# One level of Strassen's algorithm in both feed-forward stages of a chain of transformer layers

## The chip, the cores and the metric

The kernel is one program on 1 core of one Trainium2 chip. The metric is the device time of one execution in microseconds, the median of several runs. TensorE (PE) multiplies, VectorE (DVE), ScalarE (ACT) and GpSimd (POOL) compute elementwise, SyncE (SP) issues most transfers. Everything is fp32.

## The reference

Batch B = 16, T = 128 rows, width D = 512. Seven blocks follow one another: self attention, cross attention, a feed-forward stage, a grouped attention, a recurrence, an attention over latents, a second feed-forward stage. The change touches the two feed-forward stages alone, each of which is, with a hidden width of 2048:

```
x = rows of the block before                   # (16, 128, 512)
h = gelu(norm(x) @ w1 + b1)                    # (16, 128, 2048)
out = residual + h @ w2 + b2                   # (16, 128, 512)
```

The first one (`mlp`) has a layer norm and its own rows as the residual, the second (`pmlp`) an RMS norm and another tensor as the residual.

## The kernel before

Both stages are built by `mlp_phase` (L1908), called at L3282 as `mlp` and at L3298 as `pmlp`. A stage takes the 16 sequences two at a time, so it has NIT = 8 iterations; `run_iterations` writes out the first and the last and puts the six between into a loop. Each engine has its own program, with the order written out by hand; semaphores tie them together. `W1` and `W2` lie in SBUF (`region_a`) for the whole stage.

An iteration on PE (`body`, L2073): first the hidden products (L2083). For each of 16 tiles of 128 hidden features, four matmuls add up over the 512 inputs. Weights of 128x128 are the stationary operand, the 256 rows of both sequences the moving one. Two tiles share a bank, four banks go round (`Ring` `ph`). ScalarE takes each bank through gelu into `h_t` (L2013). Then PE transposes the normed rows of the next iteration (L2069), which ScalarE writes as `src_t` (L2004, `rows_features`). Then the output products (L2095): for each of the two sequences 16 matmuls with a 128x128 tile of `h_t` stationary and 512 columns of `W2` moving. VectorE adds bank and residual into `y` (L2050), SyncE stores it (`store`).

VectorE also norms the rows of the next iteration (`normalise`, L2024: statistics at L227 to L241, then L2034 or L2037), with the reciprocal root on GpSimd (L247, `rstd_on_pool`). GpSimd adds `b2` to the residual (L1986). `first.x` holds the rows of a stage's first iteration, prepared by the stage before. ScalarE starts the loads of the next stage's weights at the very beginning of a stage (L1996); those of the stage behind `mlp` go to `region_b` (`D_w`). `own_weights.wait` waits for the stage's own. Elsewhere the rows speak of the recurrence (L2915: products of 128x128 weights with 128 columns; L2404, L2700, L2714: elementwise work of GpSimd and VectorE) and of the group stage (L1764, L1801).

## Time and profile before

| | |
|---|---|
| median of 3 runs | 3412.55 us (3410.26 to 3412.62) |
| profiled execution | 3415.04 us, span 3413.3 us, mean granted TensorE clock 0.974 |
| PE busy | 3159.8 us, 93% of the span |
| VectorE, ScalarE, GpSimd busy | 1738.8, 1165.0, 865.6 us |
| `mlp` stage | about 717 to 1172 us of the span |
| `pmlp` stage | about 2957 us to the end |

In the rows, L12 is line 12 of the kernel. A group gives its engine, operation, output and inputs, shapes, count, the busy time in us, the mean duration of one in ns, and the time in which its engine stood idle ahead of it, with what ended that. Each fp32 matmul shows as two records of PE and two of PEld (the weight load). Neighbours in a pipeline overlap, so a mean duration is longer than the distance from one start to the next. PEclk is the granted TensorE clock as a share of 2.4 GHz.

### The profile page before, as it was taken

To read this page: it belongs to the slowest core of one execution; us is meant where nothing else is said; L and a number is where in the kernel's file an instruction comes from. 1 tells how busy PE (TensorE), PEld (TensorE's weight loads), DVE (VectorE), ACT (ScalarE), POOL (GpSimd) and SP (SyncE) were. 2 spreads that over 40 slices of the span, in tenths; PEclk is the share of its full clock that TensorE was granted. 3 is DMA by queue.
4 is the path that set the end of the run, shared out by engine and by line. 5 is a ranking of instruction groups with operands and counts; after the bars stand their busy time and mean duration, and the time that the engine had idled before them with its cause. 6 is when DMAs were issued, how large, how long until landed. Compare 5 with 4: busy or idle time off the path is not lost. (4 is left out here: it accounts for less than half of the span.)

```text
span 3413.3 us, 52562 instructions
## 1 busy us (share of the span) xinstructions
PE 3159.8 (93%) x19136; PEld 2073.7 (61%) x19136; DVE 1738.8 (51%) x2498; ACT 1165.0 (34%) x4115; POOL 865.6 (25%) x629
## 2 busy tenths in 40 slices
PE   8999899989999989886899999997899999899999
PEld 5665566656666655554676667664455555567675
DVE  5555455520000078884899999997344644400000
ACT  3444233431111176662343444342233433311110
POOL 3333233310000012222655555555000000100000
PEclk9999999989999999997999999998899999999999
DMA  4110231110000131111111111110231110101010
GB/s 170 43 43 27 83 130 52 40 62 25 15 22 15 42 147 53 52 33 66 45 39 41 47 50 38 44 42 29 74 125 34 38 32 24 47 22 34 22 34 12
DMA packets 104306, 170.16 MB, mean 50 GB/s; under 512 B 16512, under 2 KB 54016, under 8 KB 100736
## 3 DMA queue, kind: packets, MB, share of 16 engines
q1 hardware_dynamic: 99296, 124.58, 11.5%
q10 hardware_dynamic: 4896, 44.04, 3.2%
q8 instruction: 74, 1.21, 0.1%
q14 instruction: 40, 0.33, 0.0%
HBM read 135.03 MB, written 33.55 MB: 49 GB/s over the span
## 5 line engine op out<-in xcount | busy, mean ns | idle before, releaser
L2404 POOL TENSOR_TENSOR rec_S<-rec_S,rec_r_t 128x1024 f32<-128x1024 f32 x128 | 306.1, 2392 | 314.2 <-DVE rec_S L2729 313.2
L2729 DVE TENSOR_TENSOR_SCAN rec_S<-rec_decay,rec_S 128x1024 f32<-128x1024 f32 x128 | 299.5, 2340 | 8.2 <-DVE rec_S L2714 4.2
L2083 PE MATMUL mlp_bank<-mlp_src_t,region_a 128*128 128x256 f32 x1024 | 224.1, 381 | 3.2 <-ACT mlp_src_t L2004 3.2
L2083 PE MATMUL pmlp_bank<-pmlp_src_t,region_a 128*128 128x256 f32 x1024 | 224.6, 382 | 1.5 <-ACT pmlp_src_t L2004 1.5
L2095 PE MATMUL pmlp_bank<-region_a,pmlp_h_t 128*128 128x512 f32 x512 | 221.1, 592 | 0.0
L2095 PE MATMUL mlp_bank<-region_a,mlp_h_t 128*128 128x512 f32 x512 | 221.1, 592 | 0.0
L2083 PEld LDWEIGHTS mlp_bank<-mlp_src_t,region_a 128*128 128x128 f32 x1024 | 195.7, 191 | 33.5 <-issue 6.9
L2083 PEld LDWEIGHTS pmlp_bank<-pmlp_src_t,region_a 128*128 128x128 f32 x1024 | 196.1, 192 | 31.9 <-issue 5.2
L1510 ACT ACTIVATE group_scores<-group_scores,group_negmax 128x128 f32<-128x128 f32 x512 | 197.5, 391 | 29.6 <-DVE group_negmax L1605 19.3
L2050 DVE TENSOR_TENSOR mlp_y<-mlp_bank,mlp_xres 128x512 f32<-128x512 f32 x16 | 11.1, 692 | 374.0 <-PE mlp_bank L2095 374.0
L2050 DVE TENSOR_TENSOR pmlp_y<-pmlp_bank,pmlp_xres 128x512 f32<-128x512 f32 x16 | 11.1, 692 | 364.0 <-PE pmlp_bank L2095 364.0
L2013 ACT ACTIVATE pmlp_h_t<-pmlp_bank,vectors 128x256 f32<-128x256 f32 x128 | 53.7, 471 | 353.4 <-PE pmlp_bank L2083 353.4
L2013 ACT ACTIVATE mlp_h_t<-mlp_bank,vectors 128x256 f32<-128x256 f32 x128 | 53.8, 471 | 347.8 <-PE mlp_bank L2083 347.8
L2095 PEld LDWEIGHTS mlp_bank<-region_a,mlp_h_t 128*128 128x128 f32 x512 | 96.7, 190 | 118.7 <-issue 118.6
L2095 PEld LDWEIGHTS pmlp_bank<-region_a,pmlp_h_t 128*128 128x128 f32 x512 | 96.7, 190 | 118.7 <-issue 118.6
L608 ACT ACTIVATE latent_scores<-latent_scores,region_a 128x256 f32<-128x256 f32 x256 | 126.4, 498 | 71.7 <-DVE region_a L795 71.7
L608 ACT ACTIVATE self_scores<-self_scores,self_negmax 128x128 f32<-128x128 f32 x256 | 98.7, 389 | 76.8 <-DVE self_negmax L795 76.8
L3031 PE MATMUL rec_rec_out<-rec_S,head_sum 128*32 128x256 f32 x1024 | 83.6, 399 | 44.7 <-POOL rec_S L2404 43.6
L608 ACT ACTIVATE cross_scores<-cross_scores,cross_negmax 128x128 f32<-128x128 f32 x256 | 98.7, 389 | 76.4 <-DVE cross_negmax L795 76.4
L2714 DVE TENSOR_TENSOR rec_S<-rec_vb,rec_k 128x1016 f32<-128x1016 f32 x96 | 115.2, 1200 | 0.0
L979 PE MATMUL latent_pjA<-latent_src_t,F_query_key 128*128 128x512 f32 x240 | 114.4, 600 | 0.0
L1986 POOL TENSOR_TENSOR mlp_xres<-mlp_x,rows 128x512 f32<-128x512 f32 x16 | 20.3, 1266 | 340.8 <-DVE mlp_y L2050 329.4
(394 smaller groups left out, 6583.9 us busy)
## 6 DMA issues: line engine op xcount, KB each, us to landing
rec_vb<-v_by_head SPq DMA_DIRECT2D x32, 512.0 KB, 4.1
region_a<-in_C_w ACTq DMA_DIRECT2D x2, 4096.0 KB, 19.2
region_a<-in_G_w ACTq DMA_DIRECT2D x2, 4096.0 KB, 18.2
self_xres<-in_x SPq DMA_DIRECT2D x16, 256.0 KB, 2.6
rows_A<-self_xres SPq DMA_DIRECT2D x16, 256.0 KB, 2.0
cross_ctx_t<-in_ctx_t SPq DMA_DIRECT2D x16, 256.0 KB, 3.4
cross_xres<-rows_A SPq DMA_DIRECT2D x16, 256.0 KB, 2.6
rows_B<-cross_xres SPq DMA_DIRECT2D x16, 256.0 KB, 2.0
```

What stands on the lines that cost most here:

```text
L608: nc.scalar.activation(S[:, u, at, :], S[:, u, at, :], ACT.Exp, bias=negmax[:, u, at.start // KB:at.start // KB + 1], accum_out=rowsum[:, ...
L979: last = nc.tensor.matmul(pj.bank(item)[:, :], Wk[:, c, n * 128:n * 128 + 128], src_t[:, c, :, :], start=c == 0, stop=c == C - 1)
L1510: nc.scalar.activation(S[:, u, at, :], S[:, u, at, :], ACT.Exp, bias=negmax[:, u, at:at + 1], accum_out=rowsum[:, u // UPS, sum_column(u, ...
L1986: nc.gpsimd.tensor_tensor(xres[:, k, :], xr[:, k, :], row(cfg["b2"]), ALU.add)\
L2013: hidden = nc.scalar.activation(h_t[:, 2 * n + i, :], ph.bank(("h", n))[:, i * TT:(i + 1) * TT], ACT.Gelu_apprx_tanh, bias=vec(cfg["b1"], ...
L2050: nc.vector.tensor_tensor(y[:, k, :], po.bank(("out", k))[:, :], xres[:, k, :], ALU.add)\
L2083: product = nc.tensor.matmul(ph.bank(item)[:, i * TT:(i + 1) * TT], W1[:, c, f:f + 128], src_t[:, c, :, :], start=c == 0, stop=c == C - 1)
L2095: product = nc.tensor.matmul(po.bank(item)[:, :], h_t[:, c, k * T:k * T + T], W2[:, c, :], start=c == 0, stop=c == HC - 1)
L2404: nc.gpsimd.tensor_tensor(S[u % 4][:, :, :], S[u % 4][:, :, :], bcast(r_t[:, s.k, UNITS[u][0], :], [128, JH, T], 1), ALU.mult)\
L2714: nc.vector.tensor_tensor(S[u % 4][:, :, 1:T], vb[jh][:, :, 0:T - 1], bcast(k_bank[s.k][:, m * T:m * T + T - 1], [128, JH, T - 1], 1), ALU ...
L2729: nc.vector.tensor_tensor_scan(St[:, :, :].rearrange(flat), decay[m][:, :, :].rearrange(flat), St[:, :, :].rearrange(flat), 0.0, ALU.mult, ...
L3031: last = nc.tensor.matmul(rec_out[32 * g:32 * g + 32, jh * 2 * T:(jh + 1) * 2 * T], head_sum, S[u % 4][:, 2 * g:2 * g + 2, :], start=m == ...
```

## The change

In both stages each of the two matrix products is cut into 2 x 2 blocks, and seven products of sums of blocks take the place of the eight products of blocks (the variant with 15 sums). The blocks of the left matrix are the two sequences by the halves of the inner dimension, those of the weights the halves of both dimensions: `w11` to `w22`, `z11` to `z22`.

Hidden products: two groups `g` of 4 tiles of 128 features in each half. Each of the seven products of a group is 4 tiles x 2 inner chunks = 8 matmuls with 128 columns of moving data (one sequence), in a bank of its own (banks 1 to 7), in the order 1, 6, 7, 5, 2, 4, 3. ScalarE copies product 1 to SBUF (`copy_m1`), VectorE forms the running sums u2, u3, u4 and the four results c22, c11, c21, c12, which it writes to `h_t` as they are; ScalarE applies gelu in place. Then VectorE forms four sums of these (`h_sums`).

Output products: the seven products are 8 matmuls each, with a tile of hidden values stationary and 256 columns of weights moving. VectorE adds sums and residual into `y` in quarters.

The sums of the rows (`row_sums`) are four additions of 128x256 an iteration on VectorE. The sums of `W1` (`first_weights`, VectorE) and of `W2` (`second_weights`, GpSimd) are formed once a stage, in the first iteration; some overwrite a block of the weights, others have homes in `region_b`, at the end of `region_a`, or in new tiles. Since `region_b` is in use, `mlp` starts the loads of the next stage's weights only after the last gelu (`late_weights`). The transposed rows have one bank in place of two; the transposes of the second sequence stand behind output product 1. The diff, cut (in `product`, n is the number of the product; M[n] is its bank):

```diff
+    HB = HC // 2
+    G = 2
+    N = HB // G
+    E = D // 2
...
+        src_t = sb("src_t", [128, SL, C, T])
+        x11, x21 = src_t[:, 0, 0:2, :], src_t[:, 0, 2:4, :]
+        x12, x22 = src_t[:, 1, 0:2, :], src_t[:, 1, 2:4, :]
+        x_t1 = x12
+        HF = HID // 2
+        w11, w12 = W1[:, 0:2, 0:HF], W1[:, 2:4, 0:HF]
+        w21, w22 = W1[:, 0:2, HF:HID], W1[:, 2:4, HF:HID]
+        w_s1 = w21
+        w_s2, w_s3, w_s4 = (h.rearrange("p (c f) -> p c f", c=2) for h in (m[:, :] for m in sums[:3]))
+        z_t2, z_t3, z_t4 = (h.rearrange("p (c e) -> p c e", c=HB) for h in (m[:, :] for m in sums[3:]))
+        z11, z12 = W2[:, 0:HB, 0:E], W2[:, 0:HB, E:D]
+        z21, z22 = W2[:, HB:HC, 0:E], W2[:, HB:HC, E:D]
+        z_t1 = z12
+        h_t = sb("h_t", [128, SL, HC, T])
+        h11, h12 = h_t[:, 0, 0:HB, :], h_t[:, 0, HB:HC, :]
+        h21, h22 = h_t[:, 1, 0:HB, :], h_t[:, 1, HB:HC, :]
+        h_s1 = h21
-        ph = Ring(f"{name}_hidden", sem, banks[:4], [("h", n) for n in range(HI)])
-        px = Ring(f"{name}_rows", sem, banks[4:6], [("x", k) for k in range(SL)])
-        po = Ring(f"{name}_out", sem, banks[6:], [("out", k) for k in range(SL)])
+        M = dict(enumerate(banks[:7], 1))
...
+        px = Ring(f"{name}_rows", sem, banks[7:], [("x", k) for k in range(SL)])
...
+            def second_weights():
+                own_weights.wait(pool)
+                pool.wait_ge(w_sums, 4)
+                for g in range(2):
+                    at = slice(g * HB // 2, (g + 1) * HB // 2)
+                    nc.gpsimd.tensor_tensor(z_t3[:, at, :], z22[:, at, :], z12[:, at, :], ALU.subtract).then_inc(z_sums, 1)
+                    pool.wait_ge(z_sums, 4 * g + 1)
+                    nc.gpsimd.tensor_tensor(z_t1[:, at, :], z12[:, at, :], z11[:, at, :], ALU.subtract).then_inc(z_sums, 1)
+                    pool.wait_ge(z_sums, 4 * g + 2)
...
+                if is_first(it):
+                    second_weights()
                 if not last:
-                    norm_scale(it + 1)
+                    rstd_on_pool(nc, pool, stats, rstd, minus_half, norm_sems[2], rstd_done, it)
...
-            if next_weights:
+            if next_weights and not cfg["late_weights"]:
...
+            def copy_m1(it, chain, width):
+                act.wait_ge(m1_full, it * 3 + chain + 1)
+                wait_count(act, c11_done, it * 3 + chain)
+                nc.scalar.copy(m1[:, 0:width], M[1][:, 0:width]).then_inc(m1_copied, 1)
+            def gelu(tile, half, g):
+                for n in range(g * N, g * N + N):
+                    last = nc.scalar.activation(tile[:, n, :], tile[:, n, :], ACT.Gelu_apprx_tanh,
+                                                bias=vec(cfg["b1"], half * HB + n))
+                return last
+            def hidden(it, g):
+                chain = it * 3 + g + 1
+                copy_m1(it, g, BANK)
+                act.wait_ge(c22_done, it * 2 + g + 1)
+                gelu(h22, 1, g).then_inc(gelu22, 1)
...
+                for g in range(G):
+                    hidden(it, g)
+                if last and next_weights and cfg["late_weights"]:
+                    next_weights.start(act)
                 if not last:
                     rows_features(it + 1)
+                copy_m1(it, 2, E)
...
+            def first_weights(g):
+                at = slice(g * N * 128, (g + 1) * N * 128)
+                nc.vector.tensor_tensor(w_s3[:, :, at], w11[:, :, at], w21[:, :, at], ALU.subtract).then_inc(w_sums, 1)
+                dve.wait_ge(w_sums, 4 * g + 1)
+                nc.vector.tensor_tensor(w_s1[:, :, at], w21[:, :, at], w22[:, :, at], ALU.add).then_inc(w_sums, 1)
+                dve.wait_ge(w_sums, 4 * g + 2)
...
+            def row_sums(it):
+                for k in range(SL):
+                    dve.wait_ge(px.free_sem(("x", k)), px.uses_with(it, ("x", k)))
+                nc.vector.tensor_tensor(x_t3[:, :, :], x22, x12, ALU.subtract).then_inc(x_sums, 1)
+                dve.wait_ge(x_sums, it * 4 + 1)
+                nc.vector.tensor_tensor(x_t1, x12, x11, ALU.subtract).then_inc(x_sums, 1)
...
+            def sums_of_products(it, chain, width):
+                n = it * 3 + chain + 1
+                dve.wait_ge(m6_full, n)
+                dve.wait_ge(m1_copied, n)
+                nc.vector.tensor_tensor(u2[:, 0:width], M[6][:, 0:width], m1[:, 0:width], ALU.add).then_inc(u2_done, 1)
+                dve.wait_ge(m7_full, n)
+                dve.wait_ge(u2_done, n)
+                nc.vector.tensor_tensor(u3[:, 0:width], M[7][:, 0:width], u2[:, 0:width], ALU.add).then_inc(u3_done, 1)
...
+            def hidden(it, g):
+                n = it * 3 + g + 1
+                sums_of_products(it, g, BANK)
+                dve.wait_ge(m5_full, n)
+                dve.wait_ge(u3_done, n)
+                nc.vector.tensor_tensor(h22[:, tiles(g), :], by_tile(M[5]), by_tile(u3), ALU.add).then_inc(c22_done, 1)
+                nc.vector.tensor_tensor(u4[:, :], M[5][:, :], u2[:, :], ALU.add).then_inc(u4_done, 1)
+                if is_first(it) and g == 0:
+                    first_weights(1)
+                yield
+                dve.wait_ge(m2_full, n)
...
+                yield
+                at, now = tiles(g), it * 8 + g * 4
+                dve.wait_ge(gelu11, it * 2 + g + 1)
+                dve.wait_ge(gelu12, it * 2 + g + 1)
+                nc.vector.tensor_tensor(h_s3[:, at, :], h11[:, at, :], h21[:, at, :], ALU.subtract).then_inc(h_sums, 1)
+                dve.wait_ge(h_sums, now + 1)
+                dve.wait_ge(gelu22, it * 2 + g + 1)
...
             def body(it, last=False):
+                one, two = hidden(it, 0), hidden(it, 1)
+                next(one)
+                next(one)
+                next(one)
+                next(two)
                 if not last:
                     normalise(it + 1)
                 else:
...
+                next(two)
+                next(two)
+                if not last:
+                    row_sums(it + 1)
+                rows_out(it)
+            own_weights.wait(dve)
+            first_weights(0)
+            row_sums(0)
             run_iterations(dve, body)
...
+            def hidden(it, g):
+                def product(n, w, rows, full):
+                    for i in range(N):
+                        f = (g * N + i) * 128
+                        for c in range(2):
+                            last = nc.tensor.matmul(M[n][:, i * T:(i + 1) * T], w[:, c, f:f + 128], rows[:, c, :],
+                                                    start=c == 0, stop=c == 1)
+                    last.then_inc(full, 1)
+                chain = it * 3 + g
+                wait_count(pe, m1_copied, chain)
+                product(1, w11, x11, m1_full)
+                wait_count(pe, u2_done, chain)
+                pe.wait_ge(x_sums, it * 4 + 3)
+                if is_first(it):
+                    pe.wait_ge(w_sums, 4 * g + 3)
+                product(6, w_s2, x_t2, m6_full)
+                wait_count(pe, u3_done, chain)
+                product(7, w_s3, x_t3, m7_full)
+                wait_count(pe, u4_done, chain)
+                product(5, w_s1, x_t1, m5_full)
+                wait_count(pe, c11_done, chain)
+                product(2, w12, x21, m2_full)
+                wait_count(pe, c21_done, chain)
+                pe.wait_ge(x_sums, it * 4 + 4)
+                product(4, w22, x_t4, m4_full)
+                wait_count(pe, c12_done, chain)
+                if is_first(it):
+                    pe.wait_ge(w_sums, 4 * g + 4)
+                product(3, w_s4, x22, m3_full)
+            def rows_out(it, last):
+                def product(n, h, z, full, ready=None):
+                    for c in range(HB):
+                        if ready and c == N:
+                            pe.wait_ge(*ready)
+                        last = nc.tensor.matmul(M[n][:, 0:E], h[:, c, :], z[:, c, :], start=c == 0, stop=c == HB - 1)
+                    last.then_inc(full, 1)
+                chain, now = it * 3 + 2, it * 8 + 4
+                pe.wait_ge(m1_copied, chain)
+                pe.wait_ge(gelu11, it * 2 + 2)
+                product(1, h11, z11, m1_full)
+                if not last:
+                    transpose_rows(it + 1, 1)
+                pe.wait_ge(u2_done, chain)
+                if is_first(it):
+                    pe.wait_ge(z_sums, 8)
+                pe.wait_ge(h_sums, now)
+                product(6, h_s2, z_t2, m6_full, ready=(h_sums, now + 3))
+                pe.wait_ge(u3_done, chain)
+                product(7, h_s3, z_t3, m7_full)
+                pe.wait_ge(u4_done, chain)
+                product(5, h_s1, z_t1, m5_full)
+                pe.wait_ge(c11_done, chain)
+                pe.wait_ge(gelu21, it * 2 + 2)
+                product(2, h12, z21, m2_full)
+                pe.wait_ge(c21_done, chain)
+                pe.wait_ge(gelu22, it * 2 + 2)
+                product(4, h22, z_t4, m4_full)
+                pe.wait_ge(c12_done, chain)
+                pe.wait_ge(h_sums, now + 4)
+                product(3, h_s4, z22, m3_full)
...
+                for g in range(G):
+                    hidden(it, g)
                 if not last:
-                    transpose_rows(it + 1)
...
-            transpose_rows(0)
+                    transpose_rows(it + 1, 0)
+                rows_out(it, last)
+            for k in range(SL):
+                transpose_rows(0, k)
             run_iterations(pe, body)
...
+                               homes=[region_b[:, n * 2048:(n + 1) * 2048] for n in range(4)]
+                               + [region_a[:, 8 * C * D:8 * C * D + 2048]], late_weights=True,
...
+                           homes=[region_a[:, 8 * C * D:8 * C * D + 2048]], late_weights=False,
```

## Rows read from the trace of the kernel before

**Rows 1.** busy time of each engine, its share of the span, instructions (the page)

```profile
PE 3159.8 (93%) x19136; PEld 2073.7 (61%) x19136; DVE 1738.8 (51%) x2498; ACT 1165.0 (34%) x4115; POOL 865.6 (25%) x629
```

**Rows 2.** chain that ended last, last stage: start us, us, what; pattern repeats

```profile
2956.82 1.10 PE pmlp_bank L2069 x4
...
2960.26 30.10 PE pmlp_bank L2083 x128
...
2991.24 27.47 PE pmlp_bank L2095 x64
3018.71 27.63 PE pmlp_bank L2083 x128
3046.34 0.87 PE pmlp_bank L2069 x8
```

**Rows 3.** groups of PE: busy us, mean ns of one, idle before and its releaser

```profile
L2083 PE MATMUL mlp_bank<-mlp_src_t,region_a 128*128 128x256 f32 x1024 | 224.1, 381 | 3.2 <-ACT mlp_src_t L2004 3.2
L2095 PE MATMUL pmlp_bank<-region_a,pmlp_h_t 128*128 128x512 f32 x512 | 221.1, 592 | 0.0
```

**Rows 4.** group of DVE: the addition of L2050

```profile
L2050 DVE TENSOR_TENSOR mlp_y<-mlp_bank,mlp_xres 128x512 f32<-128x512 f32 x16 | 11.1, 692 | 374.0 <-PE mlp_bank L2095 374.0
```

**Rows 5.** group of PEld: weight loads of the output products

```profile
L2095 PEld LDWEIGHTS pmlp_bank<-region_a,pmlp_h_t 128*128 128x128 f32 x512 | 96.7, 190 | 118.7 <-issue 118.6
```

**Rows 6.** PE in order of time, recurrence: start us, us, instructions

```profile
1593.58 3.74 PE L2915 MATMUL rec_bank_d<-rec_xm,region_a 128*128 128x128 f32 x32
1597.16 3.74 PE L2915 MATMUL rec_bank_a<-rec_xm,region_a 128*128 128x128 f32 x32
1600.73 0.60 PE L2908 MATMUL rec_bank_b<-ident,rec_x 128*128 128x128 f32 x4
```

**Rows 7.** DVE in order of time: recurrence, then `normalise` of the last stage

```profile
1780.12 0.67 DVE L2692 TENSOR_TENSOR rec_bank_a<-rec_bank_a,rec_sx_t 128x512 f32<-128x512 f32 x1
1780.90 0.69 DVE L2700 TENSOR_TENSOR rec_xm<-rec_bank_a,rec_xa_t 128x512 f32<-128x512 f32 x1
1781.51 0.69 DVE L2669 BATCH_NORM_STATS2 rec_stats<-rec_x 128x6 f32<-128x512 f32 x1
...
1782.59 1.21 DVE L2714 TENSOR_TENSOR rec_S<-rec_vb,rec_k 128x1016 f32<-128x1016 f32 x1
1783.92 2.29 DVE L2729 TENSOR_TENSOR_SCAN rec_S<-rec_decay,rec_S 128x1024 f32<-128x1024 f32 x1
...
3026.15 1.29 DVE L227 BATCH_NORM_STATS2 pmlp_stats<-pmlp_x 128x6 f32<-128x512 f32 x2 [6.71 <-DMA pmlp_x<-rows_F]
...
3028.99 0.88 DVE L2034 TENSOR_SCALAR pmlp_xn<-pmlp_x,pmlp_rstd 128x512 f32<-128x512 f32 x2 [0.81 <-POOL pmlp_rstd L247]
```

**Rows 8.** ACT in order of time, last stage

```profile
3047.10 2.18 ACT L2004 ACTIVATE pmlp_src_t<-pmlp_bank,vectors 128x128 f32<-128x128 f32 x8
```

**Rows 9.** stretch: us, busy (x) of PE, PEld, DVE, ACT, POOL, PEclk, DMA, GB/s

```profile
2956.00:2964.00 8.00, 5.67 (x17) 4.62 (x18) 0.00 (x0) 3.46 (x9) 2.53 (x2) 0.50 0.42 134
```

**Rows 10.** POOL in order of time, and one row of DVE beside it

```profile
723.45 1.26 POOL L1986 TENSOR_TENSOR mlp_xres<-mlp_x,rows 128x512 f32<-128x512 f32 x1 [0.98 <-DMA mlp_x<-rows_B]
...
1786.29 2.37 POOL L2404 TENSOR_TENSOR rec_S<-rec_S,rec_r_t 128x1024 f32<-128x1024 f32 x1 [2.60 <-DVE rec_S L2729]
...
1786.13 1.19 DVE L2714 TENSOR_TENSOR rec_S<-rec_vb,rec_k 128x1016 f32<-128x1016 f32 x1
```

**Rows 11.** DMA issue: KB each, median us to landing

```profile
region_b<-in_D_wo ACTq DMA_DIRECT2D x1, 1024.0 KB, 9.9
```

**Rows 12.** pauses of PE in the group stage, and stretches around them

```profile
1367.76 1.98 PE L1764 MATMUL group_pjA<-region_b,group_o_t 128*128 128x512 f32 x4 [1.23 <-DVE group_xres L1632]
...
1523.07 0.43 PE L1801 MATMUL group_pjB<-group_probs_t,group_v 128*32 128x128 f32 x8 [2.78 <-DVE group_probs_t L1612]
...
1362.00:1372.00 10.00, 8.77 (x88) 4.59 (x80) 8.88 (x13) 4.36 (x18) 2.23 (x3) 1.00 0.00 0
1524.00:1528.00 4.00, 4.00 (x38) 2.21 (x38) 2.85 (x2) 3.74 (x19) 3.35 (x3) 0.57 0.32 119
```

150 lines of the change are left out of this document (94 added, 56 removed).

## The prediction

> **What bounds the kernel now.** I read the page's busy shares first, then the chain that ended last, then the groups of PE, then stretches in order of time. TensorE is busy 93% of the span [rows 1]. The chain of the last stage is PE and nothing else: it alternates 27.63 us of L2083 (128 records), 0.87 us of transposes and 27.47 us of L2095 (64 records) [rows 2]. Each `matmul` is two records of PE, so an iteration has 64 hidden products of 256 columns and 32 output products of 512. The groups say the same for all eight iterations, with 3.2 us idle before L2083 in all and none before L2095 [rows 3]. VectorE, by contrast, stood idle 374 us ahead of its one addition at L2050 [rows 4]. So in these two stages (about 56 us an iteration, 16 iterations) every microsecond of TensorE counts and VectorE, ScalarE and GpSimd have room. The change spends that room.
>
> **The change, part by part.** The pitch (start to start) of a record is 27.63/128 = 0.2159 us at 256 columns and 27.47/64 = 0.4292 us at 512 [rows 2].
>
> Output stage. Seven products of 8 matmuls of 256 columns are 56 matmuls = 112 records, the form that L2083 has now: 112 x 0.2159 = 24.18 us in place of 27.47, so 3.29 us less per iteration.
>
> Hidden stage. Seven products, two groups, 8 matmuls each, 128 columns: 112 matmuls = 224 records. Their columns are 7/8 of before, but each record now loads 128 columns of weights for only 128 columns of data. Two ends: by columns alone 7/8 x 27.63 = 24.18 us; by the duration of a weight load, 0.190 us (96.7 us over 512 records of L2095's loads, which overlap nothing of their own) [rows 5], 224 x 0.190 = 42.6 us. The nearest row decides: L2915 in the recurrence is exactly this form (128x128 weights, 128 columns of data, fp32), and the next groups of 32 records and what follows them begin at 1593.58, 1597.16 and 1600.73 [rows 6]. That is 3.575/32 = 0.1117 us a record, also across a boundary between banks with its semaphore waits. I take it: 224 x 0.1117 = 25.02 us, 2.61 us less. Together 5.90 us less per iteration, 47.2 per stage.
> The Trainium skill, page "TensorE: Matmul & The Clock Gate", Part 3 ("What overlaps and what doesn't"), says that a weight load overlaps running matmuls only when their row groups differ, which full 128-row products never do. With the same page's estimate of P/1.2 ns for a load, 107 ns, added to a record's stream, a record would take 0.21 us and the hidden stage 48 us. The rows of L2915 speak against it: their pitch has no room for both in turn.
>
> Where PE will wait. PE writes the products in the order 1, 6, 7, 5, 2, 4, 3, and each has a bank to itself, so a bank is wanted again a whole round (12.5 us) later; VectorE's seven additions of a round (0.69 us each alone, 0.61 apart when independent, 0.78 when one needs the last [rows 4, 7]) are 5 us, and its four sums of a gelu'd group 3 us: it keeps up. One place is tight, the start of the output stage. Product 1 there needs `gelu11` of the second group, and VectorE has `normalise` queued between the additions after product 5 and the one after product 2. I count from the end of product 5 in the second group. VectorE: two additions to 1.26, then `normalise`, which takes from 3026.15 to 3029.87 = 3.72 us with its 0.70 us on GpSimd inside [rows 7], so c11 starts at 4.9 and is done at 5.6. ScalarE: four gelus of 128 columns; eight Identities of that size take 2.18 us [rows 8], so 0.25 apart and 0.45 for the last, 1.2 us: 6.9. PE: products 2, 4, 3 are 3 x 1.787 = 5.36, one set of transposes 0.44: it is ready at 5.8. So PE pauses 1.1 us, and a restart costs 0.1 (four records of 512 columns after a pause took 1.98 us [rows 12], against 3 x 0.429 + 0.592 = 1.88 in a run [rows 2, 3]): 1.2 us in iterations 1 to 6. The last iteration has no `normalise` and no pause. After the pause, the sums h_s3, h_s1, h_s2 of the second group are there by about 11.9 and are wanted in the middle of product 6 at 12.9: covered by one microsecond, and the cover is product 1 and the transposes behind it. The pause can be nothing if something goes faster, or 2.5 us if each handoff costs 0.2 more.
>
> First iteration. `first_weights(1)`, four additions of 128x1024, is put into VectorE's queue before c11 of the first group. A 128x1016 addition takes 1.21 and its dependent starts 1.33 after it [rows 7]: 5.2 us. Followed through (c12 of group one at 8.3 after product 5, its last gelu at 10.3, four sums to 13.2, then u2, u3, c22, u4 to 16.0, `normalise` to 19.7, c11 20.3, gelus 21.6) PE, ready at 18.3, starts at 21.6: 3.4 us with the restart. `first_weights(0)` ends 5.2 us after the stage begins and x_sums some 1.2 later; PE's first transposes start at 2956.82 and product 1 at 2960.26, 3.4 us in; it takes 3.6 at the half clock (1.2 GHz) that rules there, 0.50 from 2956 to 2964 [rows 2, 9], so product 6 finds its sums ready. The two transposes of rows now share one bank, so the second waits for ScalarE: 0.6 us more ahead of the first product. GpSimd's eight sums of W2 take 2.37 each [rows 10], 19.5 us with handoffs, from about 724.7, where the residual's additions end [rows 10], done by 744; its `rstd` for the next rows is asked near 748 and the sums near 755. Covered by 4 us.
> GpSimd and VectorE then both run additions with two inputs in SBUF. In the recurrence they already do: L2404 takes 2.37 us from 1786.29 while L2714 takes 1.19 from 1786.13 [rows 10], the latter no longer than the 1.21 at 1782.59 [rows 7]. The Trainium skill, page "SBUF — State Buffer" ("Who interferes with whom"), calls the pair of ports an exclusive lock. By it the sums would run in turn and the first iteration would lose some 5 us more per stage; those two rows do not show that.
>
> What is at nothing. The weights of the group stage (two loads of 1 MB and two small) start after the last gelus instead of at the beginning. The last of them lands 9.9 us after its issue [rows 11] and the output stage behind them lasts 24 us; without that cover they would cost 10. Stores of y and loads of x: both have a stage of slack. The four issues on ScalarE's queue delay only `copy_m1`, wanted a product later. The last addition has half the columns: 0.3 us less.
>
> Sum, per stage: -47.2 + 6 x 1.2 + 3.4 + 0.6 = -36.0. Two stages and the tail: -72.3 us. The profiled execution spans 3413.3 (3415.04 by its own time); the median is 3412.55. I put the sum against each: 3341.0 of span, 3342.7 for an execution like the profiled one, 3340.2 for the median, which I forecast as 3340.
>
> **Rivals.**
> 1. The pauses drop the clock. After a pause of 2.78 us at 1523 the granted clock is 0.57 from 1524 to 1528, which is 3.4 of the 4 us at the lower level (1.2 GHz) and the rest at 2.4; around a pause of 1.23 it stays at 1.00 [rows 12]. If each iteration's pause brought one such fall, 1.7 us is lost in it, 14 x 1.7 = 24 for both stages: 3364; with falls twice as long 3388. For it: in the trace falls come after pauses of PE, and this change puts one into each iteration. Against: the 1.23 us pause, and my first-iteration pause (1.4 + 1.9 us) is the only one near 2.8; even there it is 2 to 3 us once per stage.
> 2. No pause at all, because ScalarE or `normalise` is quicker than I add up: -94.4 and 3.6 back at the starts, 3321. Against: VectorE works its queue in order and the 3.72 us stand in the trace.
> 3. Slower: loads of weights are not hidden behind 128 columns. In the hidden stage, at 0.190 us a record [rows 5], 42.6 us in place of 27.63; no pause is left, since three products then outlast VectorE's queue. (14.9 - 3.3) x 16 = +186: about 3600. It decides from 0.138 us a record upward: there (27.63 + 3.29)/224 the gain of the output stage is used up. For it: 190 ns is what one load takes, far more than the pitch. Against: rows 6, the same form at 0.1117. It would need a cause that L2915's bursts of 100 records don't have. The rule of the skill above would be this rival at 0.21 us: about +270.
> 4. The change doesn't do what it says: the program orders of the engines block one another (a VectorE queue that trails PE by more than a round), PE waits in each round for as much as it saves, and the time stays at 3412. Against: about 26 us of VectorE work (two groups of 8, `normalise` 3.7, row sums 1.6 and the output's quarters 4 to 5, by halves of 0.69 us [rows 4, 7]) in 50 us of PE.
>
> **How the numbers follow.** Forecast as summed 0.72; rival 1 0.13; rival 2 0.05; rival 3 0.07; rival 4 0.03. The forecast's own range is 3328 (half of the pauses) to 3358 (pauses of 2.2 us: 6 x 1.0 x 2 = 12, and a clock fall of 3 us in each first iteration, 6). To reach 8 in 10 it takes in most of rival 2 and the lighter half of rival 1: 3321 to 3370. A change of 0.2%, 6.8 us, is about what can be told from none. Faster 0.90, same 0.03, slower 0.07.
>
> **What would show each step.** A pitch of 0.112 us a record in the 128-column groups and 0.216 in the output groups, 1792 and 896 records per stage; one idle gap before product 1 of the output stage, ended by ScalarE's gelu, of about 1.1 us, absent in the last iteration and 3 us with the transposes in the first; iterations of 51.3 us instead of 55.97; no wait for the weights of the group stage. I am wrong if the hidden groups' pitch is over 0.12, if PE waits inside a round for VectorE, or if the granted clock in these stages falls below 0.97.

## The result and the profile after

| | before | after |
|---|---|---|
| median | 3412.59 us (3410.26 to 3414.97, 4 runs) | 3373.96 us (3371.16 to 3376.24, 4 runs) |
| profiled execution, its span | 3415.04, 3413.3 | 3371.16, 3369.4 |
| mean granted TensorE clock | 0.974 | 0.970 |
| `mlp` stage | 453.4 | 431.5 |
| `pmlp` stage | 452.2 | 429.5 |

Times are in us; a stage is counted from the start of PE's first transpose to the start of its last output product's last record, here and in the experiments. The ratio is 0.9882, interval 0.9869 to 0.9894: 38.6 us faster. The forecast was 3340 (72 us less) with a range to 3370, so the direction is right, and the size about half. Section 1 of the page of after, to be held against [rows 1]:

```profile
PE 3084.8 (92%) x21440; PEld 2242.8 (67%) x21440; DVE 2092.6 (62%) x3058; ACT 1239.9 (37%) x4419; POOL 908.0 (27%) x645
```

PE has 75 us less to do, and VectorE 354 us more. Where an iteration has settled, it looks as forecast. PE of after in order of time, `pmlp`, iterations 1 and 2 (start us, us, what, in brackets the idle time before it and what ended that); then the last two entries of the chain that ended last, which answer to [rows 2]:

```profile
3034.28 3.69 PE L2298 MATMUL pmlp_bank<-region_a,pmlp_h_t 128*128 128x256 f32 x16 [1.22 <-ACT pmlp_h_t L2087]
...
3058.97 1.95 PE L2267 MATMUL pmlp_bank<-pmlp_src_t,region_a 128*128 128x128 f32 x16
3060.75 1.95 PE L2267 MATMUL pmlp_bank<-pmlp_x_t,region_a 128*128 128x128 f32 x16
...
3083.98 0.60 PE L2258 MATMUL pmlp_bank<-ident,pmlp_xn 128*128 128x128 f32 x4
3085.79 1.53 PE L2298 MATMUL pmlp_bank<-region_a,pmlp_h_t 128*128 128x256 f32 x6 [1.22 <-ACT pmlp_h_t L2087]
...
3316.68 25.01 PE pmlp_bank L2267 x224
3341.69 24.19 PE pmlp_bank L2298 x112
```

The 224 hidden records take 25.01 us and the 112 output records 24.19: 25.02 and 24.18 were forecast. From 3034.28 to 3085.79 an iteration is 51.51 us (51.67 in `mlp`), against 55.97 before. The one idle gap in it is the 1.22 us ahead of output product 1, ended by a gelu.

The missing time lies in the first iteration of each stage. PE of after, `mlp`:

```profile
717.39 1.09 PE L2258 MATMUL mlp_bank<-ident,first_x 128*128 128x128 f32 x4 [4.06 <-PEq L194]
720.08 1.12 PE L2258 MATMUL mlp_bank<-ident,first_x 128*128 128x128 f32 x4 [1.59 <-ACT mlp_src_t L2075]
722.88 3.46 PE L2267 MATMUL mlp_bank<-mlp_src_t,region_a 128*128 128x128 f32 x16 [1.69 <-ACT mlp_src_t L2075]
729.55 5.34 PE L2267 MATMUL mlp_bank<-mlp_x_t,region_b 128*128 128x128 f32 x32 [3.21 <-DVE mlp_x_t L2153]
...
746.76 5.25 PE L2267 MATMUL mlp_bank<-mlp_x_t,region_b 128*128 128x128 f32 x32 [2.94 <-DVE region_b L2141]
...
761.20 0.63 PE L2258 MATMUL mlp_bank<-ident,mlp_xn 128*128 128x128 f32 x4 [2.04 <-DVE mlp_xn L2131]
763.56 5.31 PE L2298 MATMUL mlp_bank<-region_a,mlp_h_t 128*128 128x256 f32 x16 [1.73 <-ACT mlp_h_t L2087]
```

PE waits 3.21 us for a row sum (product 6, first group), 2.94 us for a sum of `W1` (product 6, second group), 2.04 us for the next normed rows. The first two were not forecast; of the third, 1.4 us was, as the first part of the pause put at 1.4 + 1.9. The first two answer to one sight in the rows of VectorE, and of GpSimd beside it:

```profile
720.95 2.17 DVE L2143 TENSOR_TENSOR region_b<-region_a,region_b 128x1024 f32<-128x1024 f32 x1
...
724.56 2.46 DVE L2151 TENSOR_TENSOR mlp_src_t<-mlp_src_t 128x256 f32<-128x256 f32 x1
727.05 2.44 DVE L2153 TENSOR_TENSOR mlp_x_t<-mlp_src_t 128x256 f32<-128x256 f32 x1
729.53 2.45 DVE L2155 TENSOR_TENSOR mlp_x_t<-mlp_src_t,mlp_x_t 128x256 f32<-128x256 f32 x1
733.14 0.69 DVE L2161 TENSOR_TENSOR mlp_u<-mlp_bank,mlp_m 128x512 f32<-128x512 f32 x1 [1.16 <-PE mlp_bank L2267]
...
740.07 3.26 DVE L2139 TENSOR_TENSOR region_a<-region_a 128x1024 f32<-128x1024 f32 x1
743.36 3.25 DVE L2141 TENSOR_TENSOR region_b<-region_a 128x1024 f32<-128x1024 f32 x1
746.64 1.22 DVE L2143 TENSOR_TENSOR region_b<-region_a,region_b 128x1024 f32<-128x1024 f32 x1
```

```profile
724.20 2.54 POOL L2045 TENSOR_TENSOR region_a<-region_a 128x1024 f32<-128x1024 f32 x1
726.81 2.40 POOL L2047 TENSOR_TENSOR region_a<-region_a 128x1024 f32<-128x1024 f32 x1
729.29 2.40 POOL L2049 TENSOR_TENSOR region_b<-region_a 128x1024 f32<-128x1024 f32 x1
731.77 2.42 POOL L2051 TENSOR_TENSOR mlp_w<-region_a,region_b 128x1024 f32<-128x1024 f32 x1
...
742.33 3.20 POOL L2051 TENSOR_TENSOR mlp_w<-region_a,region_b 128x1024 f32<-128x1024 f32 x1
```

A row sum of 128x256 takes 2.45 us, one GpSimd instruction long; at 3040.08, with GpSimd idle, L2151 takes 0.42. A sum of `W1` takes 3.26 in place of 1.22, and GpSimd's own go from 2.40 to 3.20. L2161, whose one operand is a PSUM bank (`mlp_bank`), takes its usual 0.69 us beside the instruction from 731.77. This looks like one engine waiting for the other, instruction by instruction, where both read two operands from SBUF; the experiments test it.

With these waits the granted clock falls from 2.4 to 1.2 GHz for a while. Stretches of after (us, then busy time and count of PE, PEld, DVE, ACT, POOL, then PEclk, DMA share, GB/s):

```profile
727.00:737.00 10.00, 7.45 (x53) 7.45 (x54) 6.59 (x6) 1.26 (x1) 9.76 (x5) 0.83 0.00 1
...
747.00:757.00 10.00, 10.00 (x79) 10.00 (x80) 7.13 (x11) 4.08 (x13) 0.00 (x0) 0.86 0.00 0
757.00:767.00 10.00, 6.23 (x33) 5.20 (x32) 6.46 (x15) 6.14 (x20) 0.70 (x1) 0.83 0.00 1
767.00:777.00 10.00, 10.00 (x50) 8.82 (x49) 4.42 (x10) 1.90 (x6) 0.00 (x0) 1.00 0.01 2
```

0.83 of full speed in 10 us is 3.4 us at the lower level. In finer steps there are three such falls in the first iteration of `mlp` (from 729.3, 746.4 and 763.4, each 3.4 us) and two in that of `pmlp` (2961.6, 3.4 us; 2978.7, 6.8 us), beyond the slow start of a stage that before has too [rows 9]. No later iteration has one.

### The profile page after: what moved, and what is told of

Its sections match the earlier page's. It is cut to its first block and busy times, and to the rows that moved or that the text cites. A ratio compares the mean times of both kernels' runs of the same rounds, so it can differ in the third digit from the quotient of the medians.

```text
span 3369.4 us, 58824 instructions
## 1 busy us (share of the span) xinstructions
PE 3084.8 (92%) x21440; PEld 2242.8 (67%) x21440; DVE 2092.6 (62%) x3058; ACT 1239.9 (37%) x4419; POOL 908.0 (27%) x645
## 5 line engine op out<-in xcount | busy, mean ns | idle before, releaser
L2087 ACT ACTIVATE mlp_h_t<-mlp_h_t,vectors 128x128 f32<-128x128 f32 x256 | 80.1, 389 | 137.0 <-DVE mlp_h_t L2171 90.2
L2087 ACT ACTIVATE pmlp_h_t<-pmlp_h_t,vectors 128x128 f32<-128x128 f32 x256 | 80.1, 389 | 135.3 <-DVE pmlp_h_t L2171 87.3
L1510 ACT ACTIVATION_READ_ACCUMULATOR group_scores<-group_scores,group_negmax 128x1 f32 x512 | 97.5, 190 | 0.0
L2298 PE MATMUL pmlp_bank<-region_a,pmlp_h_t 128*128 128x256 f32 x384 | 88.7, 389 | 9.0 <-ACT pmlp_h_t L2087 9.0
L2298 PE MATMUL mlp_bank<-region_a,mlp_h_t 128*128 128x256 f32 x384 | 87.6, 385 | 9.0 <-ACT mlp_h_t L2087 9.0
L2267 PE MATMUL mlp_bank<-mlp_src_t,region_a 128*128 128x128 f32 x768 | 92.5, 278 | 1.7 <-ACT mlp_src_t L2075 1.7
L2267 PE MATMUL pmlp_bank<-pmlp_src_t,region_a 128*128 128x128 f32 x768 | 92.8, 278 | 1.3 <-ACT pmlp_src_t L2075 1.3
L532 POOL TENSOR_TENSOR cross_scores<-cross_scores,cross_bias 128x1024 f32<-128x1024 f32 x32 | 74.8, 2360 | 69.1 <-DVE cross_scores L784 69.1
L2267 PEld LDWEIGHTS mlp_bank<-mlp_src_t,region_a 128*128 128x128 f32 x768 | 90.3, 195 | 2.4 <-ACT mlp_src_t L2075 2.1
L2267 PEld LDWEIGHTS pmlp_bank<-pmlp_src_t,region_a 128*128 128x128 f32 x768 | 90.5, 195 | 2.1 <-ACT pmlp_src_t L2075 1.7
```

What stands on the lines that cost most here:

```text
L532: nc.gpsimd.tensor_tensor(half, half, bias[:, u, :].unsqueeze(1).unsqueeze(1).to_broadcast([128, 4, 2, T]), ALU.add).then_inc(bias_added, 1)
L1510: nc.scalar.activation(S[:, u, at, :], S[:, u, at, :], ACT.Exp, bias=negmax[:, u, at:at + 1], accum_out=rowsum[:, u // UPS, sum_column(u, ...
L2087: last = nc.scalar.activation(tile[:, n, :], tile[:, n, :], ACT.Gelu_apprx_tanh, bias=vec(cfg["b1"], half * HB + n))
L2267: last = nc.tensor.matmul(M[n][:, i * T:(i + 1) * T], w[:, c, f:f + 128], rows[:, c, :], start=c == 0, stop=c == 1)
L2298: last = nc.tensor.matmul(M[n][:, 0:E], h[:, c, :], z[:, c, :], start=c == 0, stop=c == HB - 1)
```

## The experiments

Theory: the sums of `W2` on GpSimd and VectorE's sums in the first iteration exclude each other; that costs about 10 us a stage; the rest of the shortfall is the pause ahead of output product 1. Rivals: the work for `W1` on VectorE is to blame by itself; the clock falls are; something in the settled iterations is. The first four kernels ran on one chip (before 3415.3 us), the next four on a second (before 3415.9), the last three on a third (before 3414.9); each is compared with before on its own chip. Stage times come from one profiled execution each, and those of after itself differ by 1.3 and 2.5 us between two executions (431.5 and 429.5 here, 432.8 and 432.0 further down). The diffs are against after, if not said otherwise.

**Without the sums of W2.** These sums are left out; blocks of `W2` stand in.

```diff
+        z_t2, z_t3, z_t4 = z22, z22, z21
-                if is_first(it):
-                    second_weights()
...
-                if is_first(it):
-                    pe.wait_ge(z_sums, 8)
```

> The changed kernel without the eight sums of W2 on GpSimd (output products read plain blocks, so this part of the computation is left out). Theory A (VectorE's additions with two inputs in SBUF wait for GpSimd's, in the first iteration of each stage): the row sums of the first iteration fall from 2.45 to 0.43 us each and first_weights(1) from up to 3.26 to 1.23; PE's waits before product 6 (3.2 and 2.9 us) all but vanish, the one before the transposes falls to about 1; with fewer clock falls about 10 us less per stage: 3354. Theory B (the order of VectorE's queue and the clock are the cause, GpSimd is not): under 2 us per stage, 3371 to 3374.

Measured: 3349.1 us, ratio 0.9807 (0.9791 to 0.9823). The stages take 421.1 and 420.0, 10.4 and 9.5 less than in after. Here are VectorE and PE in order of time:

```profile
722.03 0.42 DVE L2152 TENSOR_TENSOR mlp_x_t<-mlp_src_t 128x256 f32<-128x256 f32 x1
...
732.08 1.23 DVE L2138 TENSOR_TENSOR region_a<-region_a 128x1024 f32<-128x1024 f32 x1
```

```profile
749.14 0.63 PE L2257 MATMUL mlp_bank<-ident,mlp_xn 128*128 128x128 f32 x4 [1.69 <-DVE mlp_xn L2130]
751.51 3.69 PE L2297 MATMUL mlp_bank<-region_a,mlp_h_t 128*128 128x256 f32 x16 [1.73 <-ACT mlp_h_t L2086]
```

The sums are short again (the first two row sums, 1.36 and 1.38, still meet GpSimd's residual additions), no product 6 waits, and of the further clock falls only one of 3.4 us is left in `pmlp`. What was put at nothing costs 20 us, both stages together.

**Without any sums of weights.** `first_weights`, `second_weights` and their waits are left out, all sums of weights are replaced by blocks.

```diff
+        w_s2, w_s3, w_s4 = w11, w11, w12
+        z_t2, z_t3, z_t4 = z22, z22, z21
...
-                if is_first(it) and g == 0:
-                    first_weights(1)
-            first_weights(0)
```

> As the run before, and without the eight sums of W1 on VectorE too (all sums of weights left out, plain blocks in their place): the first iteration has what every other one has, and the start. Theory A: its iteration takes 51.5 us and the start; another 3 us less per stage than without the W2 sums alone: 3348. Theory B (order and clock are the cause): the whole 11 us per stage that were missing come back only here, 3350.

Measured: 3343.1 us, 0.9793 (0.9777 to 0.9809), stages 418.4 and 415.7, no further clock fall. The sums of `W1` cost 2.6 and 4.3 us a stage, near the 2 allowed for them; the first rival falls. That is close to the 3340 forecast for the whole change, but here without any of its sums of weights.

**GpSimd later.** The first half of the `W2` sums waits for the row sums, the second for the sums of the first gelu'd group; PE waits for seven sums, then for the eighth.

```diff
+                    pool.wait_ge(*((x_sums, 4), (h_sums, 4))[g])
...
-                    pe.wait_ge(z_sums, 8)
+                    pe.wait_ge(z_sums, 7)
...
+                if is_first(it):
+                    pe.wait_ge(z_sums, 8)
```

> The same work as the changed kernel, but GpSimd's first four sums of W2 wait for VectorE's row sums and its last four for the four sums of the first group of hidden values; PE asks for seven of them before product 6 of the output and for the eighth before product 4. Theory A: row sums at 0.43, first_weights(1) mostly at 1.23, some 7 to 9 us less per stage: 3358, if the last W2 sums are not late for PE. Theory B: no gain, or slower by what PE waits for the later sums: 3374 or more.

Measured: 3369.9 us, 0.9865 (0.9849 to 0.9882), stages 429.6 and 429.2. No product 6 waits any more in `mlp` (one waits 0.73 us in `pmlp`), but GpSimd's `rstd` now stands behind the last four sums. GpSimd, VectorE and PE in `mlp`:

```profile
757.64 0.70 POOL L247 TENSOR_TENSOR mlp_rstd<-mlp_stats,minus_half 128x2 f32<-128x2 f32 x1
```

```profile
758.38 1.00 DVE L2132 TENSOR_SCALAR mlp_xn<-mlp_x,mlp_stats,mlp_rstd 128x512 f32<-128x512 f32 x2 [5.50 <-POOL mlp_rstd L247]
```

```profile
759.07 1.09 PE L2259 MATMUL mlp_bank<-ident,mlp_xn 128*128 128x128 f32 x4 [8.46 <-DVE mlp_xn L2132]
```

The waits were not removed but gathered into one of 8.46 us (8.42 in `pmlp`), with clock falls of 10.2 and 13.7 us around them. Moving the conflict clear of VectorE's sums is not enough: GpSimd's queue has a second customer.

**`normalise` earlier.** In iterations 1 to 6 it goes ahead of c11 of the first group, in place of after the second group's product 5.

```diff
+                if not last and not is_first(it):
+                    normalise(it + 1)
                 next(one)
...
-                if not last:
+                if is_first(it):
                     normalise(it + 1)
```

> The changed kernel with VectorE's normalise of the next rows moved, in iterations 1 to 6, from behind the additions of product 5 of the second group to the same place in the first group. Theory: c11 of the second group no longer waits for it, the pause of 1.22 us before output product 1 goes, and an iteration takes 50.1 instead of 51.5 us: 12 x 1.4 = 17 us less, 3357. Rival: the pause is ScalarE's or a handoff's, and stays over 0.8 us: 3370 to 3374.

Measured: 3355.2 us, 0.9827 (0.9811 to 0.9844), stages 420.5 and 423.3. The pause is gone:

```profile
862.66 0.60 PE L2260 MATMUL mlp_bank<-ident,mlp_xn 128*128 128x128 f32 x4
863.09 3.62 PE L2300 MATMUL mlp_bank<-region_a,mlp_h_t 128*128 128x256 f32 x16
```

A settled iteration takes 50.06 us in both stages, so pause and restart were 51.51 - 50.06 = 1.45 us in `pmlp` and 51.67 - 50.06 = 1.61 in `mlp`, 18.4 in all (1.2 and 14.4 were forecast).

**Both mended.** GpSimd's residual additions and its first four sums wait for the row sums, two for the sums of `W1`, two for those of the first gelu'd group; `normalise` as above.

```diff
+                    if g == 1:
+                        pool.wait_ge(w_sums, 8)
...
+                    if g == 1:
+                        pool.wait_ge(h_sums, 4)
...
+                if is_first(it):
+                    pool.wait_ge(x_sums, 4)
```

> The same work as the changed kernel, with normalise moved as before (iterations 1 to 6) and GpSimd's queue in the first iteration laid into VectorE's gaps: the residual's additions and the first four sums of W2 wait for VectorE's row sums, the next two for first_weights(1), the last two for the sums of the first group, so that rstd is not behind anything when it is asked. Theory (contention for SBUF operands plus the pause are what was missing): row sums 0.43, the third sum of first_weights(1) in time, PE's longest wait in the first iteration under 2 us; 19 us less per stage than the changed kernel, 75 less than the kernel before. Rival (clock falls come from somewhere else and stay): 60 to 65 less than before.

Measured: 3341.7 us (3339.7 to 3343.8), 0.9789 (0.9772 to 0.9805), stages 416.6 and 416.7. Nothing is left out here, and it beats both kernels. VectorE and PE in `mlp`:

```profile
718.25 0.42 DVE L2157 TENSOR_TENSOR mlp_src_t<-mlp_src_t 128x256 f32<-128x256 f32 x1
...
730.56 3.26 DVE L2145 TENSOR_TENSOR region_a<-region_a 128x1024 f32<-128x1024 f32 x1
733.85 1.23 DVE L2147 TENSOR_TENSOR region_b<-region_a 128x1024 f32<-128x1024 f32 x1
```

```profile
750.41 0.63 PE L2266 MATMUL mlp_bank<-ident,mlp_xn 128*128 128x128 f32 x4 [4.23 <-DVE mlp_xn L2137]
```

The expected longest wait of under 2 us did not come about: PE still waits 4.23 us for the next normed rows, 4.37 in `pmlp`. `rstd` is not to blame, it starts 0.1 us after its input is there. VectorE itself is late: one sum of `W1` is still caught (3.26, and two in `pmlp`, 2.52 and 3.25), then the first sum of the gelu'd group (1.08 in place of 0.69) and the last small step of the statistics (0.52 in place of 0.17), each beside a sum of GpSimd. The clock still falls in each first iteration, for 6.8 and 10.2 us.

**A second bank for the first rows.** On top of the one before, the rows of the second sequence are transposed into bank 7 in the first iteration.

```diff
+                bank = M[7] if is_first(it) and k == 1 else px.bank(item)
```

> As the run before, and the first rows' second sequence is transposed into the bank of product 7 instead of the shared one, so that its transposes need not wait for ScalarE. PE's wait of 1.59 us between the two goes; the first product starts 1.5 to 2 us earlier per stage: 3 to 4 us less than the run before. Rival: VectorE's first_weights(0) is then late, and the gain is under 1 us.

Measured: 3342.4 us, 0.9791 (0.9774 to 0.9807), stages 416.8 and 416.3: no gain. Product 1 starts 4.2 us into the stage in place of 5.0, but product 6 of the second group waits 1.49 us (2.07 in `pmlp`) for the third sum of `first_weights(1)`, two sums of which are caught now (2.69 and 3.26). What the start gains is lost behind it.

**Half-size sums.** After, with each of GpSimd's sums cut into two of 128x512.

```diff
+                def pieces(out, one, two):
+                    for c in range(0, out.shape[1], 2):
+                        last = nc.gpsimd.tensor_tensor(out[:, c:c + 2, :], one[:, c:c + 2, :], two[:, c:c + 2, :], ALU.subtract)
...
```

> The changed kernel with each of GpSimd's eight sums of W2 cut into two of half the size (16 of 128x512). If the two engines take turns by whole instructions (a VectorE addition with both inputs in SBUF waits for GpSimd's running one), the first row sums wait half as long, 1.3 instead of 2.45 us each, and each stage gains about 4 us: 8 less than the changed kernel. If they share the bandwidth, the row sums stay at 2.4 and nothing is gained.

Measured: 3367.3 us, 0.9864 (0.9847 to 0.988); stages 429.4 and 426.8. VectorE and GpSimd:

```profile
727.21 1.37 DVE L2158 TENSOR_TENSOR mlp_x_t<-mlp_src_t 128x256 f32<-128x256 f32 x1
```

```profile
725.44 5.67 POOL L2043 TENSOR_TENSOR region_a<-region_a 128x512 f32<-128x512 f32 x4
```

With halves of 1.42 us (5.67/4) a row sum takes 1.37 in place of 2.45: the turns go by instructions. The waits before product 6 fall to 1.71 and 0.51 us in `mlp`, but now all four of VectorE's sums of `W1` are caught (1.85 to 2.18 in place of 1.22), and two of those of the gelu'd group; the transposes, ready earlier, wait 5.95 for the normed rows, which VectorE, not GpSimd, has late. **After, run again** beside it:

> The changed kernel itself beside the others on this chip: 38 to 46 us less than the kernel before, and the row to which the other runs of this job are compared.

Measured: 3367.7 us (3362.1 to 3374.0), 0.9858 (0.9838 to 0.9879), stages 432.8 and 432.0. The halves can't be told from it by the median, since executions of after scatter by 12 us; the stages of the profiled ones are 8.6 us shorter with the halves, about the 8 us expected. That gain is not shown.

**Neither loss.** The sums of `W2` left out and `normalise` early, both edits as above.

> Both losses taken out at once: the sums of W2 are left out, as in the run without them (z_t2, z_t3, z_t4 stand for blocks of W2), and normalise is moved as in the run with the early normalise. Theory, the two losses are independent: the pause of 1.22 and its restart are worth 1.45 us in each of 12 iterations, so 17.4 off the 3349.1 of the run without the sums: 3331.7 us, ratio 0.9754, steady iterations of 50.06 us, stages of about 412. Rival, they share a cover (without the pause VectorE's queue is tight and PE waits elsewhere, or the clock falls more): less than half of it is gained, 3340 or more. What the spread version (3341.7) still pays for the sums of W2 is then its distance to this run: 10 us by the theory.

Measured: 3332.7 us, 0.9755 (0.9737 to 0.9772), stages 412.8 and 412.9, settled iterations 50.06. The two losses are independent: 16.4 us under the run without the sums of `W2`, where 17.4 were expected. The version with both mended, 3341.7, is 9 us above it (12 by the ratios): that is what it still pays for the sums of `W2`.

This run also shows what a clock fall costs by itself. Its first iterations are those of the run without the sums of `W2`, with the same waits of PE in `mlp` (1.71 and 1.73 us, there 1.69 and 1.73), but here one fall of 3.4 us comes with them, from 751.1, and there none. PE of this run, to be held against 751.51 there:

```profile
750.59 5.38 PE L2299 MATMUL mlp_bank<-region_a,mlp_h_t 128*128 128x256 f32 x16 [1.73 <-ACT mlp_h_t L2086]
```

The same 16 records take 5.38 us in place of 3.69, and the first iteration 63.45 in place of 62.11: about half of the 3.4 us is lost.

**One operand at GpSimd.** The eight instructions for `W2` take one block times 1.0, their differences are left out, all waits are kept.

```diff
-                    nc.gpsimd.tensor_tensor(z_t3[:, at, :], z22[:, at, :], z12[:, at, :], ALU.subtract).then_inc(z_sums, 1)
+                    nc.gpsimd.tensor_scalar(z_t3[:, at, :], z22[:, at, :], 1.0, None, ALU.mult).then_inc(z_sums, 1)
...
```

> GpSimd's eight instructions for W2 become products of one block with 1.0: as many elements out, one operand in SBUF in place of two; the differences of W2 are thereby left out. All waits are kept. Theory one, the two engines exclude one another whenever VectorE reads two operands from SBUF, whatever GpSimd does: the row sums still last as long as one GpSimd instruction each (about 2.4 us if the product takes as long as the sum, less if it is shorter), first_weights(1) is stretched too. Theory two, both must read two operands: row sums of 0.43 us, first_weights(1) of 1.22, PE does not wait before product 6 in the first iteration, time as without the sums, 3349 (0.981).

Measured: 3356.7 us, 0.9827 (0.981 to 0.9843), stages 424.1 and 423.2. VectorE and GpSimd in `mlp`:

```profile
723.89 1.14 DVE L2151 TENSOR_TENSOR mlp_src_t<-mlp_src_t 128x256 f32<-128x256 f32 x1
725.07 0.42 DVE L2153 TENSOR_TENSOR mlp_x_t<-mlp_src_t 128x256 f32<-128x256 f32 x1
725.53 0.43 DVE L2155 TENSOR_TENSOR mlp_x_t<-mlp_src_t,mlp_x_t 128x256 f32<-128x256 f32 x1
```

```profile
723.63 2.87 POOL L2045 TENSOR_SCALAR region_a<-region_a 128x1024 f32<-128x1024 f32 x1
```

Neither theory is right as written. While one GpSimd instruction runs from 723.63 to 726.50, two row sums go through at their own 0.42 us, and one is held up by 0.72 us; two more VectorE instructions later (at 735.95 and 744.96) are held up by 0.71 and 0.72, and two of GpSimd's 2.77 become 3.53 and 3.15. So with one operand there is still a toll, but not for the whole instruction. PE's wait before product 6 is 0.20 us and none (0.66 and none in `pmlp`).

**One operand at VectorE.** The mirror of it: row sums and `W1` sums are left out, one block times 1.0 in their place; GpSimd as in after.

```diff
-                nc.vector.tensor_tensor(x_t1, x12, x11, ALU.subtract).then_inc(x_sums, 1)
+                nc.vector.tensor_scalar(x_t1, x12, 1.0, None, ALU.mult).then_inc(x_sums, 1)
...
```

> The mirror of it: VectorE's row sums (in all iterations) and the sums of W1 become products of one block with 1.0, the sums themselves are left out, GpSimd's sums of W2 stay as they are. Theory, two operands in SBUF at VectorE are what is excluded: the products keep their own duration beside GpSimd (a quarter to 0.43 us for 128x256, under 1.23 for 128x1024), no wait of PE before product 6, GpSimd's sums stay at 2.4 instead of 3.2, time 3345 to 3352. Rival, everything of VectorE that lies in SBUF only is excluded: the 128x256 products still take about 2.4 us each and the time stays within 3 us of the changed kernel.

Measured: 3361.4 us (3355.9 to 3364.9), 0.9846 (0.9829 to 0.9862), stages 429.4 and 425.8. VectorE beside GpSimd and, at 768, alone:

```profile
724.94 2.38 DVE L2153 TENSOR_SCALAR mlp_x_t<-mlp_src_t 128x256 f32<-128x256 f32 x1
...
768.47 0.29 DVE L2153 TENSOR_SCALAR mlp_x_t<-mlp_src_t 128x256 f32<-128x256 f32 x1
```

My theory fell, and of the rival the durations held: 0.29 us of work still takes 2.38. By the ratio the time is some 4 us under the run of after above (0.9846 against 0.9858), which is inside the intervals. So a one-operand form of VectorE can be caught like the addition. But not every instruction that has all its data in SBUF is. In the run "GpSimd later" VectorE's statistics fell beside GpSimd's sums:

```profile
750.50 2.35 POOL L2048 TENSOR_TENSOR region_a<-region_a 128x1024 f32<-128x1024 f32 x1
```

```profile
750.69 1.27 DVE L227 BATCH_NORM_STATS2 mlp_stats<-mlp_x 128x6 f32<-128x512 f32 x2
...
752.41 0.46 DVE L241 TENSOR_SCALAR mlp_stats<-mlp_stats 128x2 f32<-128x2 f32 x1
```

L227 reads one operand from SBUF and writes to SBUF. Beside GpSimd's sum it takes the 1.27 us that it takes in after with GpSimd idle (at 757.80). L241, a product, takes 0.46 where it takes 0.17 there (at 759.52), and ends with GpSimd's instruction. Caught are additions with two operands in SBUF and the one-operand `tensor_scalar`; not caught are additions with one operand in PSUM and the statistics.

## Why the prediction was right and wrong

**Right: the settled iteration.** The pitch of 0.1117 us a record, taken from [rows 6], gives 25.02 us where 25.01 were measured; 0.2159 gives 24.18 where 24.19 were. The last iteration has no pause. Rival 3 (loads of weights not hidden) is out. Out with it is the estimate of 0.21 us a record, worked out from the rule of the Trainium skill, page "TensorE: Matmul & The Clock Gate", Part 3 ("What overlaps and what doesn't"), that a weight load overlaps running matmuls only when their row groups differ: the measured 0.1117 decides. Rival 1 did not come true as put, a fall of the clock in each iteration: settled iterations have none, as [rows 12] with its pause of 1.23 us at 1.00 suggested. Rival 4 (no gain) did not come true, nor did rival 2, though the early `normalise` shows that its 50 us iteration can be had. The late loads of the group stage's weights cost nothing: `D_wo` is issued at 1127.2, 25 us before that stage's first product at 1152.8.

**Mis-sized: the pause.** Forecast 1.1 + 0.1 us, measured 1.22 + 0.23 = 1.45 in `pmlp` and 1.21 + 0.40 = 1.61 in `mlp`. In 12 iterations that is 4 us more.

**The step that failed: "First iteration", its last paragraph.** My own sign of being wrong, that PE waits inside a round for VectorE, came true there. I put GpSimd's sums of `W2` beside VectorE's at no cost, by [rows 10]: L2404 on GpSimd, and L2714 on VectorE at its normal 1.19 us. These rows could not bear that. L2714 reads `rec_S<-rec_vb,rec_k`, and `rec_k` is a PSUM bank (`k_bank` in the code), so it has one operand in SBUF, like L2161 above, which is not held up either. The row sums and `first_weights` have both. I looked at duration and count of inputs and not at where each input lives. The rule I set aside is that of the Trainium skill, page "SBUF — State Buffer", "Who interferes with whom": the pair of ports shared with GpSimd is an exclusive lock, and a VectorE instruction with two SBUF inputs, or one in a two-port mode, contends for it. The measured 2.45 us for a sum of 0.42 agree, and so do L2161 and L227, which are not held up. The run with one operand at VectorE agrees as well, as far as its product at 0.69 us for 128x1024, against 1.22 for the addition, runs at about double rate, as such a mode would; which mode it ran in no trace says. Its "whole instruction" nearly holds against GpSimd's two-operand sums, and not against its one-operand products, beside which row sums ran at 0.42: there the trace decides.

The price, read from the traces. From the first transpose to iteration 1's first product the first iteration takes 72.5 us in `mlp` (717.39 to 789.87) and 71.4 in `pmlp` (2936.03 to 3007.45), where before it was 63.0 (716.95 to 779.91) and 61.9 [rows 2]. Forecast was 1.9 less than before (-5.9 + 3.4 + 0.6), so 11.4 us are missing in either:

| term, us | forecast | `mlp` | short | `pmlp` | short |
|---|---|---|---|---|---|
| waits before product 6, both groups | 0 | 3.21 + 2.94 | 6.2 | 1.78 + 2.13 | 3.9 |
| wait for the next normed rows | 1.4 | 2.04 | 0.6 | 3.97 | 2.6 |
| wait for the gelu, with restart | 2.0 | 1.73 | -0.3 | 1.68 | -0.3 |
| later start of product 1 | 0.6 | 0.3 | -0.3 | 1.3 | 0.7 |
| rest | | | 5.2 | | 4.5 |

The rest is the clock. In the first iteration PE works 14.7 us at the lower level in `mlp`, where before it was 5.5, and 14.8 in `pmlp`, where it was 6.5; at half speed that is 4.6 and 4.2 us lost, an estimate that the fall priced by itself in "Neither loss" bears out. Against the run without the sums of `W2` the first iterations are 10.4 and 9.5 us longer: 6.5 and 6.1 are more waiting of PE, 3.7 and 3.2 the lower clock. So the rival that blamed the clock falls holds for a third of the cost, and those falls come with waits that go when the sums go.

So 22.8 us of the first iterations and 4 of the pauses are missing, 26.8 of the 28.5 by which the profiled execution (3371.2) lies above the 3342.7 forecast for it. The group stage took 379.2 us where it was 377.3, but it lay between 376.8 and 379.6 in all the kernels, so I count that as chance. Nothing else of size is left. The medians are 34 apart because after's lies 2.8 above its profiled execution and before's 2.5 below.

The experiments agree in size, within the few us by which stages scatter: without the sums of `W2` the stages are 19.9 us shorter, without those of `W1` another 6.9, where the forecast had nothing and about 4.

**The range.** It was built from the pauses and one fall of the clock per stage. A rule that was weighed at 5 us a stage and had no row clearly against it should have had a chance and a place in it: 10 us on top of its end at 3370 would have taken in the result. The 5 us were themselves half of the price: with them the forecast would have been 3350, still 24 short.

## What to carry to other kernels

Before work is spread over VectorE and GpSimd, look at where each operand lives: beside GpSimd's two-operand sums in SBUF, VectorE's additions with both operands in SBUF, and its product with a constant there, wait for their turn; those with an operand in PSUM, and the statistics with one input, go on. A row that is to prove "no contention" must match in that, and not only in size. When a one-time preparation is put into a stage's first iteration, follow every customer of the engine that does it (here `rstd`), and every instruction of the other engine that it will then meet, or the wait only moves.

## What the runs showed of the hardware

- Beside a two-operand SBUF addition on GpSimd (2.40 us for 128x1024), a VectorE addition with two operands in SBUF waits for its turn: 0.42 us becomes 2.45 (1.37 beside halves of 1.42), 1.22 becomes 3.26. Additions with one operand in PSUM keep their 0.69 us, and BATCH_NORM_STATS2, with one operand in SBUF, its 1.27.
- GpSimd pays less than VectorE's work. Its sums start 2.43 us apart alone, 2.48 with a row sum of 0.42 between them, and 3.3 with an addition of 1.22: by these distances some 0.4 us of each GpSimd sum don't keep VectorE out, which is an estimate.
- A product with one operand is slower on GpSimd than the addition (2.77 against 2.35 to 2.40 us for 128x1024), but holds VectorE's two-operand additions up by 0.7 us at most, and not each time.
- VectorE's product with a constant in SBUF takes 0.69 us for 128x1024 and 0.29 for 128x256, where the addition takes 1.22 and 0.42; it is held up all the same.
- fp32 products with 128x128 weights and 128 columns run at 0.1117 us a record over a whole iteration, 256 columns at 0.2159. Half the width thus costs 3% more per column (0.2234), and the 0.190 us of a load show in neither.
- Waits of 1.2 us of PE in each of six iterations left the granted clock at 2.4 GHz, and so did the one of 1.78 in after's `pmlp`. With those of 3.21, 2.94, 2.13 and 2.04 us in after (1.73 more right behind the last) it fell to 1.2 GHz for 3.4 us each, with the one of 3.97 for 6.8, and with one of 8.46 us in "GpSimd later" for 10.2. Waits alike can differ: 1.7 and 1.73 us brought a fall in one run and none in another.
